# A fused patch, attention and FFN kernel: another order of turns and PSUM banks, and the repeating table for every turn

## The chip, the cores and the metric

The kernel runs on one core of one Trainium2 chip. The metric is the device time of a run in microseconds (us). TensorE is PE in the profile, VectorE is DVE, ScalarE is ACT, GpSimd is POOL, and SP is the engine that issues all DMAs of this kernel.

## The reference

64 images go through three parts, in float32 except where integers are imitated:

```python
h = conv2d(x, stem_w, stem_b, 4)                 # 84x84 -> 21x21, 96 channels
h = leaky_relu(batchnorm(h, ...))
offset = conv2d(h, off_w, off_b, 4)              # 16 taps x (y, x) for 25 positions
h = deform_conv(h, offset, dcn_w, dcn_b)         # bilinear samples, 192 channels
h = leaky_relu(batchnorm(h, ...))                # 25 tokens of 192
h = concatenate([h, txt], axis=1)                # 25 + 77 = 102 tokens an image
h = h + attn(layernorm(h))                       # 12 heads of 16, int8 values,
                                                 # integer log2 softmax over 102 keys
h = h + gelu(layernorm(h) @ w_in.T + b) @ w_out  # 192 -> 768 -> 192
```

The integer softmax quantises the scores, subtracts the maximum, splits each into a quotient and a remainder, forms `(r*(r+b)+c) * 2**(30-q)`, sums over the keys, and replaces each ratio sum/value by the next power of two.

## The kernel before, in words

The work is cut into *turns*. A turn is one stage of one image, or, for the stages named in `PER_GROUP`, of one group of four images. All data lives in SBUF in one or two copies, so a group is also the unit in which buffers are reused. The stages used below, with the line of their main instruction in the kernel before:

- PE: STEM0 and STEM1 (stem convolution of images 0, 1 and 2, 3 of a group, L1255), HTT (transpose, L1264), OFF and OFS (offsets, L1280, L1289), HAT (the distances of pixels to sample points, two matmuls into two banks, L1302), INT (interpolation, L1312 to L1316), DCN (L1331), LN1X and LN2X (transposes of the normalised tokens, L1345), V0, V1, FQ0, FQ1 (projections, L1355 to L1389), SC (scores, L1401, L1404), PV2 (probabilities times values, L1415), PV3 (output projection, L1425), FFN0 to FFN2 (first FFN matmuls, L1367, L1371), FF2 (second, L1452).
- ACT: an eviction under the name of the PE stage (STEM L723, HAT L755 and L760, LN1X L779, SC L839, PV2 L865, FQ L827 and L829), XH1 and XH2 (normalise, L798), SQ (square of the remainder, L846), LOG (L852) and PR (exp, L859) of the ratio, and FFN (GELU, L873), which stands between two table loads (L709).
- DVE: HAT (L1032) and HATW (L1039) turn distances into weights; LS1, LN1, VE1 and LS2, LN2, VE2 are the two layer norms; QKC casts queries and keys (L1086 to L1090); the softmax of an image is MAX (L1097), MXB, MXC, DST (L1121), BND, QQ, QQG, REM, EP, EXP (L1164), SUM (L1172), RCP (L1177), and, after ACT, PW (L1187) and PR (L1194); PV3 and RES give the residual (L1200, L1207); FF2 adds the FFN (L1214).
- POOL: NRM multiplies an image's exponentials by the reciprocal of their sum (L674, from RCP to LOG), OFS splits offsets into bf16 parts (L658 to L668), RS1 and RS2 are the reciprocal square roots of the layer norms (L683 to L686), WDF scales the convolution weights once (L651).
- SP: LX, LA, LR load, RP spreads the offsets to the rows that HAT reads (L603), SD packs samples (L593), PT transposes the probabilities (L587), QD places the queries in twelve DMAs (L578), YO0 and YO1 store.

In what follows NRM.2 is the turn of the third image of a group, RCP.2 its reciprocal, and so on; in the tables the number behind the point is an image of 0 to 63, and a group stage bears its last image.

Each engine walks the same text, `SLOT`: one entry per turn, with the engine, the stage and a lag in images; `run_slot` executes those of its engine for image `slot - lag`. So the order of the turns on each engine repeats every four images, and engines meet through semaphores alone. Two further tables, `OPENING` and `CLOSING`, list by hand the first and the last turns of each engine; `walk` runs those lists and leaves their turns out of the repeating part. `BANKS` gives each stage its PSUM banks, and `BankUse.take` makes PE wait until the stage that used a bank before has been evicted:

```python
def take(self, t, k, drained, per, plus=None):
    b = t.banks[k]
    if b in self.last:
        before, at = self.last[b]
        self.pe.wait_ge(before, at)
    self.last[b] = (drained, per * t.n + (per if plus is None else plus + 1))
```

Of the kernel before, what the change touches and what calls it, by code (L numbers as in the profile page):

```python
# [79 lines left out]
act.LOG.18 dve.RES.61 pe.HAT.7 dve.HATW.52 act.HAT.11 dve.LN2A.60 act.XH1.15 pe.FF2.18 dve.LS2.61  # L80
act.XH1.14 sp.PT.88 dve.PV3.60 pe.STEM0.0 pool.RS2.52 act.PR.18 dve.RES.60 dve.LS2.60 act.STEM.7
pe.LN1X.11 dve.LN2.60 act.LN1X.15 dve.VE2.60 pe.FF2.17 act.SQ.16 dve.MAX.59 dve.MXB.59 act.XH1.13
pe.LN1X.10 dve.MXC.59 sp.QD.84 act.LN1X.14 dve.DST.59 pe.HAT.6 act.XH1.12 dve.BND.59 act.STEM.6
pe.LN1X.9 dve.MAX.58 dve.QQ.59 pool.NRM.51 act.LN1X.13 pe.FF2.16 dve.MXB.58 act.HAT.10 dve.QQG.59
act.LOG.17 pe.LN1X.8 dve.MXC.58 sp.SD.80 dve.REM.59 act.LN1X.12 pe.PV2.15 dve.DST.58 act.PR.17
dve.EP.59 act.LOG.16 pe.V0.8 dve.BND.58 act.V.15 dve.MAX.57 pe.FQ0.8 dve.QQ.58 act.PR.16 dve.EXP.59
act.PV2.19 pe.FQ1.8 pool.OFS.40 sp.YO0.92 dve.QQG.58 act.FQ0.12 dve.EP.58 pe.PV2.14 dve.PREP0.4
act.FQ1.12 dve.REM.58 pe.HTT.3 act.OC.19 dve.SUM.59 act.V.14 dve.PREP2.52 pe.HAT.5 act.HAT.9
dve.MXB.57 sp.LR.84 dve.RCP.59 pe.PV3.15 act.PV2.18 dve.EXP.58 act.OC.18 dve.SUM.58 pe.INT.7
act.HAT.8 pool.NRM.50 dve.MXC.57 dve.MAX.56 pe.HAT.4 act.PV2.17 dve.DST.57 act.INT.11 pe.PV2.13  # L90
dve.BND.57 act.OC.17 sp.YO1.92 dve.QQ.57 pe.PV3.14 act.HTT.7 dve.QQG.57 dve.PREP3.52 act.INT.10
pe.INT.6 dve.MXB.56 act.PV2.16 dve.RCP.58 pe.PV3.13 act.OC.16 dve.REM.57 dve.LS1.55 act.SC.15
pool.RS1.44 pe.PV2.12 dve.LS1.54 sp.LX.72 act.STEM.5 dve.LS1.53 pe.INT.5 act.HTT.6 dve.LS1.52
act.STEM.4 dve.LN1.52 pe.PV3.12 dve.VE1.52 act.XH2.19 dve.EP.57 pe.SC.11 act.SC.14 dve.PREP1.16
act.XH2.18 dve.MXC.56 pe.STEM1.0 sp.DCN.80 dve.DST.56 act.INT.9 dve.BND.56 pe.HTT.2 act.VC.15
pool.NRM.49 dve.PW.59 act.INT.8 dve.FF2.63 pe.SC.10 act.LN2X.19 dve.QQ.56 dve.EXP.57 pe.INT.4
act.XH2.17 dve.QQG.56 act.SC.13 sp.LA.80 pe.LN2X.15 dve.PR.59 act.SQ.15 dve.FF2.62 pe.SC.9
# [15 lines left out]


OPENING = dict(
    pe="""
  STEM0.3 STEM1.3 HTT.0 HTT.1 OFF.3 OFS.3 HAT.0 STEM0.7 HTT.2 STEM1.7 HAT.1 HAT.2 HTT.3 HTT.4 HAT.3
  INT.0 INT.1 INT.2 INT.3 OFF.7 HTT.5 DCN.3 OFS.7 HTT.6 HAT.4 STEM0.11 LN1X.0 LN1X.1 HTT.7 HAT.5
  LN1X.2 LN1X.3 V0.3 FQ0.3 FQ1.3 STEM1.11 HAT.6 HTT.8 HAT.7 INT.4 INT.5 SC.0 SC.1 INT.6 SC.2 INT.7
  OFF.11 HTT.9 SC.3 OFS.11 DCN.7 V1.3 HTT.10 HAT.8 HTT.11 STEM0.15 HAT.9 LN1X.4 LN1X.5 LN1X.6 PV2.0  # L120
  LN1X.7 V0.7 FQ0.7 FQ1.7 PV2.1 HAT.10 HTT.12 PV3.0 INT.8 HAT.11 PV2.2 PV3.1 INT.9 PV3.2 PV2.3
  INT.10 PV3.3 SC.4 HTT.13 STEM1.15 SC.5 INT.11 LN2X.0 SC.6 LN2X.1 HTT.14 OFF.15 LN2X.2 V1.7 HTT.15
  LN2X.3 OFS.15 SC.7 DCN.11 FFN0.3
    """,
    act="""
  STEM.0 STEM.1 STEM.2 HTT.0 STEM.3 OFF.3 OFS.3 HAT.0 HTT.1 STEM.4 STEM.5 HAT.1 HTT.2 HTT.3 HAT.2
  HAT.3 INT.0 STEM.6 INT.1 HTT.4 INT.2 STEM.7 INT.3 OFF.7 DCN.3 OFS.7 HTT.5 HTT.6 HAT.4 XH1.0 STEM.8
  XH1.1 LN1X.0 XH1.2 LN1X.1 XH1.3 LN1X.2 HAT.5 LN1X.3 V.0 HTT.7 FQ0.3 STEM.9 V.1 FQ1.3 STEM.10 HAT.6
  HAT.7 INT.4 SC.0 SC.1 INT.5 INT.6 STEM.11 SC.2 INT.7 HTT.8 VC.0 SQ.0 OFF.11 OFS.11 HTT.9 SQ.1
  DCN.7 SC.3 HTT.10 LOG.0 V.2 VC.1 HAT.8 PR.0 SQ.2 V.3 HTT.11 STEM.12 LOG.1 XH1.4 XH1.5 STEM.13  # L130
  LN1X.4 PR.1 XH1.6 LN1X.5 SQ.3 LN1X.6 XH1.7 HAT.9 PV2.0 LN1X.7 VC.2 LOG.2 PR.2 LOG.3 V.4 PR.3 VC.3
  FQ0.7 FQ1.7 OC.0 V.5 HAT.10 PV2.1 OC.1 HAT.11 PV2.2 OC.2 INT.8 PV2.3 HTT.12 OC.3 INT.9 SC.4 VC.4
  STEM.14 HTT.13 STEM.15 SC.5 VC.5 XH2.0 XH2.1 INT.10 LN2X.0 INT.11 XH2.2 XH2.3 LN2X.1 SC.6 HTT.14
  LN2X.2 OFF.15 SQ.4 V.6 HTT.15 LN2X.3 SQ.5 V.7 VC.6 DCN.11 VC.7 SC.7
    """,
    dve="""
  PREP0.3 PREP1.3 HAT.0 HATW.0 HAT.1 HATW.1 HAT.2 HAT.3 HATW.2 HATW.3 PREP2.3 PREP3.3 LS1.0 LS1.1
  LS1.2 LS1.3 LN1.3 VE1.3 QKC.3 HAT.4 HATW.4 HAT.5 HATW.5 HAT.6 HATW.6 HAT.7 HATW.7 MAX.0 MXB.0
  MXC.0 DST.0 MAX.1 BND.0 MXB.1 QQ.0 MXC.1 QQG.0 DST.1 EP.0 BND.1 REM.0 QQ.1 MAX.2 QQG.1 MXB.2 EXP.0
  REM.1 SUM.0 EP.1 RCP.0 EXP.1 SUM.1 MXC.2 DST.2 BND.2 MAX.3 QQ.2 MXB.3 QQG.2 RCP.1 REM.2 LS1.4  # L140
  LS1.5 LS1.6 LS1.7 LN1.7 VE1.7 EP.2 MXC.3 DST.3 EXP.2 BND.3 PW.0 QQ.3 PR.0 QQG.3 EP.3 REM.3 SUM.2
  PW.1 RCP.2 EXP.3 SUM.3 RCP.3 PR.1 HAT.8 PW.2 PR.2 HATW.8 PW.3 PR.3 HAT.9 QKC.7 PV3.0 HAT.10 HATW.9
  RES.0 PV3.1 HAT.11 RES.1 LS2.0 HATW.10 LS2.1 PV3.2 RES.2 HATW.11 PV3.3 RES.3 LS2.2 LS2.3 LN2.3
  VE2.3 MAX.4 MXB.4 MXC.4 DST.4 MAX.5 BND.4 MXB.5 QQ.4 MXC.5 EP.4 QQG.4 DST.5 REM.4 BND.5 MAX.6 QQ.5
  MXB.6 QQG.5 EXP.4 REM.5 EP.5 SUM.4 EXP.5 RCP.4 SUM.5
    """,
    pool="""
  OFS.3 WDF.3 OFS.7 RS1.3 OFS.11 NRM.0 NRM.1 RS1.7 NRM.2 NRM.3 RS2.3 NRM.4
    """,
    sp="""  # L150
  LX.3 RP.3 LX.7 SD.3 LX.11 DCN.3 LA.3 RP.7 QD.3 SD.7 LR.3 RP.11 DCN.7 LA.7 LX.15 PT.0 PT.1 PT.2
  PT.3 QD.7 SD.11 DCN.11 LA.11 LX.19 LR.7
    """,
)
# [1380 lines left out]
```

## Time and profile before

| | us |
|---|---|
| median of 3 runs | 990.5 (989.36 to 991.37) |
| time of the profiled execution | 989.57 |
| its span, from first to last instruction | 987.5 |
| busy: PE, DVE, ACT, POOL | 844.2, 845.0, 777.5, 255.2 |
| mean granted TensorE clock, as a share of full speed | 0.958 |

A timeline row gives the start, the duration, the engine, the line, the operation and its tiles, and in brackets how long the engine had been idle and who ended that. Rows of the chain of waits give start, duration and what the chain went through. A duration of PE or DVE includes time in which the instruction had been issued and was held.

### The profile page before, as it was taken

The numbers are of one execution on the slowest core, as the hardware profiler recorded it, in microseconds if no ns is written. First come the engines' busy times: TensorE is split into PE (matmuls) and PEld (weight loads), VectorE is DVE, ScalarE is ACT, GpSimd is POOL, SyncE is SP. The second block draws the span as 40 slices with busy tenths as digits, with TensorE's granted clock in tenths as the row PEclk, the third lists the DMA queues.
The fourth block names the chain that finished last, engine by engine and source line by source line (L and its number), as shares of the span: only waits on it lengthen the run. The fifth ranks groups of instructions, "written<-read, shape, count | busy, mean of one in ns | idle before, by whom it ended". The sixth has DMA issues, their size and how long they took to land. (4 is left out here: it accounts for less than half of the span.)

```text
span 987.5 us, 18275 instructions
## 1 busy us (share of the span) xinstructions
PE 844.2 (85%) x5578; PEld 520.1 (53%) x5578; DVE 845.0 (86%) x1703; ACT 777.5 (79%) x1529; POOL 255.2 (26%) x248
## 2 busy tenths in 40 slices
...
## 3 DMA queue, kind: packets, MB, share of 16 engines
...
## 5 line engine op out<-in xcount | busy, mean ns | idle before, releaser
L674 POOL TENSOR_TENSOR ee_sb<-ee_sb,rs_sb 128x1020 f32<-128x1020 f32 x64 | 143.1, 2238 | 346.9 <-DVE rs_sb L1177 346.9
L1452 PE MATMUL bank<-w_out_sb,ge_sb 128*102 128x192 f32 x768 | 140.0, 333 | 23.5 <-ACT ge_sb L873 19.8
L1316 PE MATMUL bank<-hats_sb,ht_sb 127*96 127x400 f32 (+1 forms) x384 | 146.7, 520 | 0.4 <-ACT samp_sb L767 0.4
L1452 PEld LDWEIGHTS bank<-w_out_sb,ge_sb 128*102 128x102 f32 x768 | 121.9, 170 | 39.0 <-ACT ge_sb L873 29.5
L1039 DVE SCALAR_TENSOR_TENSOR hats_sb<-hats_sb 126x1600 f32<-126x1600 int32 x64 | 116.0, 1815 | 0.2
L760 ACT ACTIVATE hats_sb<-bank 126x400 int32<-126x400 f32 (+1 forms) x256 | 108.0, 520 | 0.0
L839 ACT ACTIVATE a_sb<-scores,sc_sb 128x1020 f16<-128x1020 f32 x64 | 71.0, 1110 | 46.3 <-PE scores L1404 46.3
L1164 DVE SCALAR_TENSOR_TENSOR ee_sb<-sq_sb,sc_sb,ep_sb 128x1020 f32<-128x1020 f32 x64 | 100.0, 1562 | 3.9 <-ACT sq_sb L846 3.9
L1316 PEld LDWEIGHTS bank<-hats_sb,ht_sb 127*96 127x96 f32 (+1 forms) x384 | 58.7, 166 | 68.7 <-issue 66.6
L846 ACT ACTIVATE sq_sb<-rm_sb,sc_sb 128x1020 f32<-128x1020 f16 x64 | 73.5, 1149 | 18.3 <-DVE rm_sb L1149 18.1
L1367 PE MATMUL bank<-xt_sb,w_in_sb 128*128 128x408 f32 (+1 forms) x204 | 83.5, 535 | 1.4 <-ACT xt_sb L779 1.4
L1121 DVE SCALAR_TENSOR_TENSOR m_sb<-a_sb,mx_sb 128x1020 f16<-128x1020 f16 x64 | 79.9, 1249 | 1.1
L1172 DVE TENSOR_REDUCE ss_sb<-ee_sb 128x10 f32<-128x1020 f32 x64 | 77.5, 1210 | 1.0
L852 ACT ACTIVATE ee_sb<-ee_sb 128x1020 f32<-128x1020 f32 x64 | 67.9, 1062 | 10.9 <-POOL ee_sb L674 10.8
L683 POOL TENSOR_TENSOR xshift_sb<-mv_sb,xshift_sb 102x4 f32<-102x4 f32 (+1 forms) x33 | 8.6, 260 | 262.5 <-DVE ve_sb L1079 261.1
L1345 PE MATMUL bank<-ident_sb,xh_sb 102*128 102x102 f32 x256 | 49.7, 278 | 23.6 <-ACT xt_sb L779 19.3
L859 ACT ACTIVATE rr_sb<-ee_sb 128x1020 uint16<-128x1020 f32 x64 | 68.3, 1067 | 1.7 <-DVE p_sb L1187 1.1
L1331 PE MATMUL bank<-wdcn_sb,samp_sb 128*100 128x192 f32 x384 | 65.1, 326 | 0.0
L873 ACT ACTIVATE ge_sb<-bank,b_in_sb 128x408 f32<-128x408 f32 (+1 forms) x102 | 51.9, 580 | 14.4 <-PE bank L1371 14.0
L1331 PEld LDWEIGHTS bank<-wdcn_sb,samp_sb 128*100 128x100 f32 x384 | 61.3, 167 | 0.0
L779 ACT ACTIVATE xt_sb<-bank 128x204 f32<-128x204 f32 x128 | 44.3, 346 | 18.7 <-PE bank L1345 18.6
L1345 PEld LDWEIGHTS bank<-ident_sb,xh_sb 102*128 102x128 f32 x256 | 31.3, 149 | 51.9 <-ACT xh_sb L798 31.5
...
## 6 DMA issues: line engine op xcount, KB each, us to landing
...
q_sb<-qb_sb SPq DMA_DIRECT2D x192, 12.8 KB, 1.9
...
```

Of the source, the lines that this page charges most:

```text
L674: nc.gpsimd.tensor_tensor(EE[b][:], EE[b][:], RS[b][:].unsqueeze(2).to_broadcast([128, RT, TOK]), ALU.mult).then_inc(scaled_done, 1)
L760: nc.scalar.activation(HATS[t.i][0:rows, 1 + j, :].bitcast(i32), bank[t.banks[1]][0:rows, 0:SMP], ACT.Abs, scale=ONE_Y, bias=-line * ONE_Y ...
L846: nc.scalar.activation(SQ[:], RM[:], ACT.Square, bias=sc[:, NHALFB:NHALFB + 1]).then_inc(sq_done, 1)
L1039: v.scalar_tensor_tensor(hat[:, 1:, :], hat[:, 1:, :].bitcast(i32), -ONE_Y, hat[:, 0:1, :].to_broadcast([rows, NCH, SMP]), ALU.add, ALU.mu ...
L1121: v.scalar_tensor_tensor(M16[b][:], A16[b][:], MAGIC16 + 128.0, MX[b][:].unsqueeze(2).to_broadcast([128, RT, TOK]), ALU.min, ALU.subtract) ...
L1164: v.scalar_tensor_tensor(EE[b][:].rearrange("p h k -> p (h k)"), SQ[:], sc[:, CC:CC + 1], EP[:].bitcast(bf16), ALU.add, ALU.mult).then_inc ...
L1172: v.tensor_reduce(SS[b][:], EE[b][:], AX.X, ALU.add).then_inc(ss_done, 1)
L1316: last = mm(dst, HT[0:rows, t.i, j, :], HATS[t.i][0:rows, 1 + j, :], start=(j == 0 and not odd), stop=(j == NCH - 2 and odd == 1))
L1331: last = mm(dst, SAMP[:, k, :, :].rearrange("c g p -> c (g p)"), WD[:, k, :], start=False, stop=(k == PACKED - 1))
L1345: last = nc.tensor.transpose(bank[t.banks[0]][:, c * TOK:(c + 1) * TOK], xh[b][:, 64 * c:64 * c + 128], ident[0:TOK, 0:TOK])
L1367: mm(bank[t.banks[first + c]][:, 0:n], weights(k + c, c), src[:, c, :], start=True, stop=False)
L1452: last = mm(bank[t.banks[0]][0:TOK, 0:D], GE[:, f, t.i * TOK:(t.i + 1) * TOK], WOUT[:, f, :], start=(f == 0), stop=(f == FT - 1))
```

## The change

`OPENING`, `CLOSING`, `turns_of` and `run_turn` go. `walk` runs only the repeating table, from the first slot to the last, so the first and last turns come in its order too. The table itself is another one, and so are the banks:

```diff
 SLOT = """
-dve.PR.62 act.V.16 pe.HTT.4 dve.FF2.64 act.LN2X.21 dve.HAT.55 pe.LN2X.17 act.VC.16 dve.PW.61
...
+dve.DST.59 act.V.14 pe.PV2.23 dve.BND.59 act.OC.18 dve.MAX.58 pe.LN1X.19 act.PV2.17 dve.QQ.59
...
-BANKS = dict(FFA=(0, 1, 2, 3), STEM0=(3, 2), STEM1=(2, 1), HTT=(5,), OFF=(3,), OFS=(0,),
-             HAT=(3, 0), INT=(4, 3), DCN=(3,), LN1X=(1,), LN2X=(1,), V0=(3, 4), V1=(4, 2),
-             FQ0=(0, 5), FQ1=(3, 1), PV2=(2,), PV3=(1,), FFN0=(4, 5), FFN1=(2, 1), FFN2=(0, 3),
-             FF2=(5,))
+BANKS = dict(FFA=(2, 0, 1, 5), STEM0=(5, 4), STEM1=(0, 1), HTT=(3,), OFF=(4,), OFS=(2,),
+             HAT=(0, 3), INT=(2, 4), DCN=(4,), LN1X=(5,), LN2X=(1,), V0=(0, 4), V1=(0, 5),
+             FQ0=(3, 5), FQ1=(0, 2), PV2=(1,), PV3=(5,), FFN0=(3, 2), FFN1=(4, 5), FFN2=(0, 1),
+             FF2=(2,))
...
-def run_slot(engine, slot, stages, apart):
+def run_slot(engine, slot, stages):
     for of_engine, stage, lag in PHASES[slot % GRP]:
-        n = slot - lag
-        if of_engine == engine and 0 <= n < IMG and (stage, n) not in apart:
-            run_turn(engine, stage, n, stages)
+        n, per_group = slot - lag, stage in PER_GROUP
+        if of_engine == engine and 0 <= n < IMG:
+            stages[stage](Turn(n // GRP if per_group else n, n % GRP, per_group,
+                               BANKS.get(stage)))
...
-    opening, closing = turns_of(OPENING, name), turns_of(CLOSING, name)
-    for stage, n in opening:
-        run_turn(name, stage, n, stages)
     for slot in range(FIRST_SLOT, LAST_SLOT + 1):
-        run_slot(name, slot, stages, {*opening, *closing})
-    for stage, n in closing:
-        run_turn(name, stage, n, stages)
+        run_slot(name, slot, stages)
```

In a few stages the waits in front of one instruction are written in another order (`xt1`, `xt2`, `quotient`, `exp_int`, `pixels_first`, `interpolate`, `weigh_v`), and PE's `stem` waits for its pixels only behind the wait for its first bank. No instruction that computes or moves data is added or removed.

PE around the first scores of a group, in the middle of the program. Before (L1425 is PV3, L1401 and L1404 are SC, L1255 is STEM1):

```order
L1415 MATMUL bank<-pt_sb,v_sb 32x102 x12
L1316 MATMUL bank<-hats_sb,ht_sb 96x400 x3
L1425 MATMUL bank<-wproj_sb,o_sb 102x192 x3
L1401 MATMUL scores<-kk_sb,q_sb 128x102 x7
L1404 MATMUL scores<-kk_sb,q_sb 128x102 x4
L1255 MATMUL bank<-xc_sb,stem_w_sb 96x441 x2
```

Now:

```order
L1313 MATMUL bank<-pt_sb,v_sb 32x102 x12
L1162 MATMUL bank<-ident_sb,h_sb 126x96 x4
L1214 MATMUL bank<-hats_sb,ht_sb 96x400 x3
L1299 MATMUL scores<-kk_sb,q_sb 128x102 x7
L1302 MATMUL scores<-kk_sb,q_sb 128x102 x4
L1323 MATMUL bank<-wproj_sb,o_sb 102x192 x3
L1153 MATMUL bank<-xc_sb,stem_w_sb 96x441 x2
```

The output projection of the group's last image, PV3.3, has moved from in front of the scores SC.0 to behind them.

ACT behind the GELUs, in the middle of the program. Before (L846 is SQ.2, L852 LOG.1, L755 and L760 HAT.0, L798 XH1.0 and XH1.1, L859 PR.1, L723 STEM.0, L779 LN1X.0, and L846 SQ.3):

```order
L846 ACTIVATE sq_sb<-rm_sb,sc_sb 128x1020
L852 ACTIVATE ee_sb<-ee_sb 128x1020
L755 ACTIVATE hats_sb<-bank 126x400
L760 ACTIVATE hats_sb<-bank 126x400 x4
L798 ACTIVATE xh_sb<-xa_sb,xshift_sb,rstd_sb 102x192 x2
L859 ACTIVATE rr_sb<-ee_sb 128x1020
L723 ACTIVATE h_sb<-bank 96x441
L779 ACTIVATE xt_sb<-bank 128x2x102
L846 ACTIVATE sq_sb<-rm_sb,sc_sb 128x1020
```

Now:

```order
L743 ACTIVATE sq_sb<-rm_sb,sc_sb 128x1020
L651 ACTIVATE hats_sb<-bank 126x400
L656 ACTIVATE hats_sb<-bank 126x400 x4
L619 ACTIVATE h_sb<-bank 96x441
L749 ACTIVATE ee_sb<-ee_sb 128x1020
L695 ACTIVATE xh_sb<-xa_sb,xshift_sb,rstd_sb 102x192 x2
L756 ACTIVATE rr_sb<-ee_sb 128x1020
L674 ACTIVATE xt_sb<-bank 128x2x102
L743 ACTIVATE sq_sb<-rm_sb,sc_sb 128x1020
```

The stem eviction STEM.0 has moved from behind XH1.0, XH1.1 and PR.1 to in front of them and of LOG.1; the turns between the two squares are the same.

POOL at the start of the program, behind its fills. Before:

```order
L658 TENSOR_TENSOR offp_sb<-offt_sb,later_sb 96x100
L661 TENSOR_TENSOR offr_sb<-offt_sb,offp_sb 96x100
L663 TENSOR_TENSOR offp_sb<-offr_sb,later_sb 96x100
L668 TENSOR_TENSOR offs_sb<-offr_sb,offp_sb 96x100
L651 TENSOR_TENSOR wdcn_sb<-wdcn_sb,ee_sb 128x2304
```

Now:

```order
L547 TENSOR_TENSOR wdcn_sb<-wdcn_sb,ee_sb 128x2304
L554 TENSOR_TENSOR offp_sb<-offt_sb,later_sb 96x100
L557 TENSOR_TENSOR offr_sb<-offt_sb,offp_sb 96x100
L559 TENSOR_TENSOR offp_sb<-offr_sb,later_sb 96x100
L564 TENSOR_TENSOR offs_sb<-offr_sb,offp_sb 96x100
```

The one scaling of the convolution weights, WDF, has moved ahead of the first group's offsets.

## Rows read from the trace of the kernel before

**Rows 1.** Windows by stage: busy us and count of each engine, clock, DMA share.
```profile
core 0: us, PE busy (x) PEld busy (x) DVE busy (x) ACT busy (x) POOL busy (x), PEclk, DMA share, GB/s
0.00:120.00 120.00, 76.58 (x392) 40.18 (x392) 74.21 (x151) 48.58 (x109) 26.55 (x38) 0.91 0.24 61
241.00:783.00 542.00, 499.14 (x3446) 311.48 (x3447) 508.90 (x1010) 476.84 (x945) 149.93 (x140) 1.00 0.26 57
...
900.00:987.00 87.00, 57.53 (x317) 38.21 (x317) 43.18 (x101) 45.41 (x73) 11.63 (x13) 0.74 0.14 30
```

**Rows 2.** Chain of waits, two groups four apart (start, us, what).
```profile
603.62 0.89 PE bank L1371 x4
...
820.45 0.89 PE bank L1371 x4
```

**Rows 3.** Chain of waits within one group.
```profile
666.09 1.15 ACT sq_sb L846
...
673.65 2.90 DVE ee_sb L1164
...
683.65 1.33 SPq L587
...
692.77 1.86 DMA q_sb<-qb_sb
```

**Rows 4.** Timeline of PE around the first scores.
```profile
693.83 0.41 PE L1425 MATMUL bank<-wproj_sb,o_sb 128*102 128x192 bf16 x3
694.67 0.49 PE L1401 MATMUL scores<-kk_sb,q_sb 128*128 128x102 bf16 x7 [0.43 <-DMA q_sb<-qb_sb]
```

**Rows 5.** Timeline of DVE from RCP.2 to HAT.0.
```profile
673.29 0.21 DVE L1177 RECIPROCAL rs_sb<-ss_sb 128x10 f32<-128x10 f32 x1
673.65 2.89 DVE L1164 SCALAR_TENSOR_TENSOR ee_sb<-sq_sb,sc_sb,ep_sb 128x1020 f32<-128x1020 f32 x1 [0.16 <-ACT sq_sb L846]
...
678.24 0.35 DVE L1214 TENSOR_TENSOR y_sb<-bank,x_sb 102x192 f32<-102x192 f32 x1
678.51 1.79 DVE L1032 TENSOR_SCALAR hats_sb<-hats_sb 126x400 f32<-126x400 f32 x1
```

**Rows 6.** Timeline of POOL, the same stretch: NRM.2 and NRM.3.
```profile
673.58 1.89 POOL L674 TENSOR_TENSOR ee_sb<-ee_sb,rs_sb 128x1020 f32<-128x1020 f32 x1 [7.56 <-DVE rs_sb L1177]
678.13 1.95 POOL L674 TENSOR_TENSOR ee_sb<-ee_sb,rs_sb 128x1020 f32<-128x1020 f32 x1 [2.66 <-DVE rs_sb L1177]
```

**Rows 7.** Line L1164 in ten groups: ns minimum, median, maximum.
```profile
L1164 DVE SCALAR_TENSOR_TENSOR ee_sb<-sq_sb,sc_sb,ep_sb x40: 1210/1273/2894, 269.3 to 781.8; 128x1020 f32<-128x1020 f32 x40
```

**Rows 8.** Timeline of DVE in the opening, the same turns.
```profile
129.96 0.21 DVE L1177 RECIPROCAL rs_sb<-ss_sb 128x10 f32<-128x10 f32 x1
130.08 1.22 DVE L1164 SCALAR_TENSOR_TENSOR ee_sb<-sq_sb,sc_sb,ep_sb 128x1020 f32<-128x1020 f32 x1
...
133.26 2.05 DVE L1032 TENSOR_SCALAR hats_sb<-hats_sb 126x400 f32<-126x400 f32 x1
```

**Rows 9.** Timeline of ACT from XH1.0 to SQ.3.
```profile
670.00 1.01 ACT L798 ACTIVATE xh_sb<-xa_sb,xshift_sb,rstd_sb 102x192 f32<-102x192 f32 x2
...
671.82 0.54 ACT L723 ACTIVATE h_sb<-bank 96x441 f32<-96x441 f32 x1
672.24 0.35 ACT L779 ACTIVATE xt_sb<-bank 128x204 f32<-128x204 f32 x1
672.46 1.16 ACT L846 ACTIVATE sq_sb<-rm_sb,sc_sb 128x1020 f32<-128x1020 f16 x1
```

**Rows 10.** Timeline of the first 75 us: offsets, weights, first HAT.
```profile
20.93 0.35 POOL L658 TENSOR_TENSOR offp_sb<-offt_sb,later_sb 96x100 bf16<-96x100 f32 x1 [4.38 <-ACT offt_sb L746]
...
22.64 1.69 SPq L603 DMA_DIRECT2D rx_sb<-offs_sb  x2
...
25.72 5.04 POOL L651 TENSOR_TENSOR wdcn_sb<-wdcn_sb,ee_sb 128x2304 f32<-128x2304 f32 x1 [3.11 <-DVE dcn_bias_parts_sb L951]
...
30.94 0.59 PE L1302 MATMUL bank<-rx_sb,lines_sb 9*126 9x400 bf16 x2 [10.53 <-DMA rx_sb<-offs_sb]
...
40.54 0.37 DVE L1032 TENSOR_SCALAR hats_sb<-hats_sb 126x400 f32<-126x400 f32 x1
```

**Rows 11.** Timeline of DVE in the opening: the wait for the first queries and keys.
```profile
86.03 0.58 DVE L1086 CAST qb_sb<-qk_sb 128x816 bf16<-128x816 int8 x1 [14.16 <-ACT qk_sb L829]
```

**Rows 12.** Timeline of DVE in the last group: EXP.61.
```profile
924.11 1.28 DVE L1164 SCALAR_TENSOR_TENSOR ee_sb<-sq_sb,sc_sb,ep_sb 128x1020 f32<-128x1020 f32 x1 [1.99 <-ACT sq_sb L846]
```

More of the change, by code:

```diff
@@ L80 @@
[L80 to L97, printed above, removed]
```

149 lines of the change are left out of this document (39 added, 110 removed).

## Prediction

> **What bounds the kernel now.** I read the windows first. In ten full groups, from 241 to 783 us, DVE is busy 508.90 us, PE 499.14 and ACT 476.84 of 542 [rows 1]: 50.9, 49.9 and 47.7 us in a group. The chain of waits then gives the length of a group: it passes the same FFN matmuls at 603.62 and, four groups on, at 820.45 [rows 2], so 216.83 / 4 = 54.2 us. No engine is full; what sets 54.2 is a loop through all of them. The reader is to see its stations within one group [rows 3]: the GELUs end, ACT squares image 2's remainder at 666.09, DVE forms EXP.3 at 673.65, the last PR turn of the group ends and SP issues the transpose PT at 683.65, then the twelve query DMAs, the last of which lands at 692.77 + 1.86 = 694.6. PE starts the scores at 694.67, 0.43 us after it had become free [rows 4]; they lead through PE's turns to the next FFN matmuls.
>
> The second thing to see is inside DVE's time. EXP takes 1.27 us as a rule, but 2.89 at 673.65 [rows 5], and of 40 in ten groups the median is 1.273 and the maximum 2.894 [rows 7]. The slow one was issued at 673.65, just behind NRM.2 on POOL at 673.58 [rows 6]. HAT.0, at 678.51, takes 1.79 us against 0.37 in the opening [rows 5, 10], and it lies under NRM.3, from 678.13 to 680.08 [rows 6]. So where DVE starts second it is held until POOL is done: 2.89 - 1.27 = 1.6 and 1.79 - 0.37 = 1.4 us, both on the loop. In the opening the same turns stand tighter: RCP.2 at 129.96, EXP.3 at 130.08 with 1.22 us, because EXP started first and POOL waited [rows 8].
> That POOL and DVE hold each other up by order of start is also what the Trainium skill says (SBUF — State Buffer, Who interferes with whom): whoever issues first keeps the shared port pair for the whole instruction and the other fully blocks. By that rule, and the trace agrees with its 2.89 against 1.22 us, a DVE turn that gets in front does not make the conflict vanish but hands it to POOL.
>
> **The change, part by part.** As many instructions of each kind run as before; only order, banks and the places of waits differ. Most of the table is the old one: the groups lag each other by the same number of rounds on every engine. I work through what moved on the loop, per group.
>
> 1. *PV3.3 behind SC.0 on PE.* It lengthens PE's way from the scores to the FFN by its own 0.41 us [rows 4]. Before, it lay in front of a 0.43 us wait for the queries and cost nothing. Behind it on DVE wait PV3.3's scaling, RES.3, LS2.3, the moments and the variance; these 1.9 us no longer fill the time in which DVE awaits SC.0. DVE has about 1 us of waits to give (0.31, 0.50 and 0.16 us in that group, the last one in [rows 5]), so it becomes late by some tenths at RCP.0, and NRM.0, LOG.0 and the GELUs with it. Bounds: 0 (if another turn holds the GELUs anyway) to 1.3 us (the whole way through DVE). I take 0.5, near PE's row, since both ways end in the same GELU.
>
> 2. *STEM.0 in front of LOG.1 and XH1.0 on ACT.* XH1.0, and with it LN1X.0, FF2.2 and RCP.2, comes later by one stem eviction, by start to start 672.24 - 671.82 = 0.42 us [rows 9]. Cost +0.4. SQ.3 does not come later, since the same turns lie between SQ.2 and SQ.3.
>
> 3. *What 2 does to EXP.3.* Before, RCP.2 started at 673.29 and SQ.3 was done at 673.62, so EXP.3 started 0.36 us behind RCP.2, and NRM.2 had come 0.07 us before it [rows 5, 6, 9]. Now RCP.2 is 0.42 later against SQ.3. The square is done 0.33 - 0.42 = 0.1 us ahead of RCP.2, and EXP.3 follows 0.12 us behind the start of RCP.2, as in the opening [rows 8], ahead of POOL, which came 0.29 us behind it. From RCP.2 to the end of the HAT turn it was 680.30 - 673.29 = 7.01 us [rows 5]; in the opening, without FF2.3, it was 135.31 - 129.96 = 5.35 [rows 8]; with FF2.3's 0.27, by start to start [rows 5], 5.62. Gain 1.4 us. The HAT turn there is now HAT.1 and is held just as HAT.0 was. Bounds: 0 (still held) to 1.6 (the whole hold). NRM.2 is late by the 1.1 us that EXP.3 keeps it, yet LOG.2 and LOG.3 stand behind HAT.1 on ACT and are not reached earlier.
>
> 4. *STEM0 and HAT.0 ahead of FF2.0 on PE, LX ahead of SD on SP, QKC directly behind PR.3, HAT.0 earlier on DVE.* STEM0 and HAT.0 now fill the time in which PE awaits the GELUs. QD waits for the transpose at 683.65 [rows 3] and not for QKC, so QKC gains nothing. LX's two issues fall into time in which SP waits for samples. Zero each. What costs it if that cover goes: PE's 1.0 us for STEM0, once a group.
>
> 5. *Banks.* LN1X gets bank 5, HTT bank 3, FF2 bank 2. I went through each bank's previous user; every one is evicted before PE comes, except HAT.1's, which waits for HAT.0's evictions about where PE would otherwise wait for XH1.0. Zero.
>
> A group: +0.5 + 0.4 - 1.4 = -0.5 us. I take -0.4, since the two orders of start must hold every time. The middle has about 14 such groups: -5.6 us.
>
> 6. *Opening.* WDF now stands ahead of the first offsets on POOL. It can't start before 25.72 and takes 5.04 us, to 30.8; the four offset turns (20.93 to 22.6) come after it, to 32.5; RP's issue of 1.69 ends at 34.2 [rows 10]. In the second group the rows land 2.3 us after such an issue, so the first HAT matmul comes at 36.5 to 36.8 instead of 30.94: +5.8. Most of it is covered: DVE takes up HAT.0 only at 40.54, behind its own constants [rows 10]. What is left is the fourth image's chain, with HTT.4, HTT.5 and STEM1 now ahead of INT.3: about +2 us on the first tokens. Against that HAT.4 and HATW.4, behind QKC before, fall into DVE's 14.16 us wait [rows 11]: up to 2.2 us. Sum +1.5; bounds -1 and +5.8.
>
> 7. *Closing.* EXP.61 waited 1.99 us for a square that stood behind GELUs in the list [rows 12]; in the table the square comes first, but the GELUs later. The last four FF2 turns wait for each other's adds as before. I take -0.5, bounds -2.5 and +3.
>
> **Sum.** 989.57 - 5.6 + 1.5 - 0.5 = 985.0 us. The profiled execution lies 0.9 us under the median of 990.5 and within the runs' spread; I leave the number as it is.
>
> **The rivals.**
>
> *A, slower: EXP.3 stays second.* If SQ.3 comes 0.3 us later against RCP.2 than I reckon (the 0.29 us between RCP.2 and NRM.2 less the 0.12 of EXP.3, plus 0.1), NRM.2 is first again and the 1.4 us are not won, while 1 and 2 are paid: +0.9 us in each of 14 groups. Place: DVE at RCP.2. 989.57 + 12.6 + 1.5 - 0.5 = 1003 us. For it: the margin is small and was missed by 0.07 us before. Against it: the opening shows the other order in this very kernel [rows 8]. Chance 0.32.
>
> *B, a wash: the opening is not covered.* Then the 5.8 us of 6 arrive whole: 989.57 - 5.6 + 5.8 - 0.5 = 989.3. For it: the clock is at 0.91 of full speed in the first 120 us [rows 1], so the later start may meet slow matmuls. Against it: DVE's start at 40.54. Chance 0.19.
>
> *C, faster still: 1 costs nothing and PE's filled wait is a gain of its own.* Then a group saves 0.4 - 1.4 = -1.0: 989.57 - 14 + 1 = 976.6. For it: PE stands idle before FF2.0 and before SC.0 in every group. Against it: the loop goes through ACT there. Chance 0.12.
>
> **How the numbers follow.** The forecast, 985.0 with a range of its own of 980 to 989, has the remaining 0.37. No change means within 0.2%, 2 us, about what a measurement of this kernel can tell. Of the forecast's case 0.33 lie under 988.5 and 0.04 above; C gives 0.12 faster; B splits 0.03, 0.11, 0.05; A gives 0.02 same and 0.30 slower. Sums: faster 0.48, same 0.17, slower 0.35. The range reaches from C's time to just over A's, 976 to 1004; beyond it lie sums of several errors.
>
> **What would show it.** In the changed profile: the chain's period between equal FFN rows, 53.8 if right, 55.1 for A, 53.2 for C. L1164's counterpart with a maximum near 1.3 us instead of 2.9, and NRM.2 rows of 2.8 us in place of 1.9. DVE idle in front of the PV3.3 scaling by 1 to 2 us in each group. The first HAT matmul near 36.7 us, and the first SC within 2 us of where it was (97.98). I am wrong if EXP.3 keeps its 2.9 us, if the period moves by more than 1 us, or if opening and closing together move by more than 4 us.

## The result, and the profile after

The changed kernel takes 976.43 us (median of 4 runs, 975.82 to 977.48) against 990.93 (4 runs), a ratio of 0.9853 with a 95% interval of 0.9838 to 0.9867. That is faster by 14.5 us; I had forecast 5.5. The profiled execution took 977.03 us with a span of 974.9, 12.5 us under the one before.

The windows of the profile after, as [rows 1] before:

```profile
0.00:120.00 120.00, 71.37 (x396) 38.43 (x396) 76.08 (x156) 49.49 (x110) 26.92 (x38) 0.84 0.24 62
241.00:783.00 542.00, 502.78 (x3509) 314.71 (x3507) 499.92 (x1021) 488.26 (x967) 167.25 (x140) 1.00 0.28 59
...
900.00:975.00 75.00, 51.45 (x274) 34.06 (x274) 39.43 (x82) 41.99 (x69) 13.16 (x12) 0.77 0.13 29
```

In the same 542 us more instructions run on PE, DVE and ACT, and yet DVE is busy 9 us less: its holds went. POOL is busy 17 us more for the same 140 instructions: it is the one that is held now.

The chain of waits, two equal stations (DCN) four groups apart, as [rows 2]:

```profile
588.93 3.90 PE bank L1229 x24
...
802.06 3.90 PE bank L1229 x24
```

213.13 / 4 = 53.3 us a group. Line L1061 (EXP), ten groups, as [rows 7]:

```profile
L1061 DVE SCALAR_TENSOR_TENSOR ee_sb<-sq_sb,sc_sb,ep_sb x40: 1219/1274/1278, 266.9 to 770.7; 128x1020 f32<-128x1020 f32 x40
```

The maximum fell from 2894 to 1278 ns: no EXP is held any more. The timeline of DVE from RCP.2 on, as [rows 5] (L1074 is RCP, L1061 EXP.3, L929 HAT.1, L1084 PW.2):

```profile
664.01 0.20 DVE L1074 RECIPROCAL rs_sb<-ss_sb 128x10 f32<-128x10 f32 x1
664.14 1.22 DVE L1061 SCALAR_TENSOR_TENSOR ee_sb<-sq_sb,sc_sb,ep_sb 128x1020 f32<-128x1020 f32 x1
...
667.58 1.78 DVE L929 TENSOR_SCALAR hats_sb<-hats_sb 127x400 f32<-127x400 f32 x1
669.78 0.43 DVE L1084 TENSOR_SCALAR p_sb<-rr_sb 128x1020 bf16<-128x1020 uint16 x1 [0.42 <-ACT rr_sb L756]
```

And POOL, as [rows 6]: NRM.2 and NRM.3 in one row.

```profile
664.30 4.84 POOL L570 TENSOR_TENSOR ee_sb<-ee_sb,rs_sb 128x1020 f32<-128x1020 f32 x2 [4.86 <-DVE rs_sb L1074]
```

EXP.3 starts 0.13 us behind RCP.2 and 0.16 us ahead of NRM.2, and takes 1.22 us; the two NRM take 4.84 us together, where they took 1.89 and 1.95. HAT.1, which lies under NRM.3, is held as HAT.0 was. The last row of DVE is new: DVE waits for ACT there. The timeline of ACT shows why, from SQ.2 to the last PR (first, middle and last rows; between them ACT never waits):

```profile
656.41 1.15 ACT L743 ACTIVATE sq_sb<-rm_sb,sc_sb 128x1020 f32<-128x1020 f16 x1
657.46 0.48 ACT L651 ACTIVATE hats_sb<-bank 126x400 f32<-126x400 f32 x1
...
668.64 1.11 ACT L756 ACTIVATE rr_sb<-ee_sb 128x1020 uint16<-128x1020 f32 x1
669.59 1.11 ACT L749 ACTIVATE ee_sb<-ee_sb 128x1020 f32<-128x1020 f32 x1
...
670.74 1.11 ACT L756 ACTIVATE rr_sb<-ee_sb 128x1020 uint16<-128x1020 f32 x1
```

From these timelines I took one start in each group: the eviction of SC.0, SQ.2, RCP.2, the last PR turn on DVE (PR.3), and the next SC.0. Means over ten groups, the fourth to the thirteenth, in us:

| kernel | SC.0 to SQ.2 | SQ.2 to RCP.2 | RCP.2 to PR.3 | PR.3 to SC.0 | group |
|---|---|---|---|---|---|
| before | 24.79 | 7.20 | 9.91 | 12.52 | 54.42 |
| changed | 24.90 | 7.60 | 8.76 | 12.25 | 53.52 |

Over the whole run: the first SC.0 is evicted at 98.78 us before and 97.59 after, the last at 908.62 and 896.50, and the span ends at 987.5 and 974.9. So the opening gained 1.2 us, the fifteen groups between 10.9, and the closing 0.4. By stretch, summed over the fifteen groups: SC.0 to SQ.2 grew by 0.9 us, SQ.2 to RCP.2 by 6.1, RCP.2 to PR.3 shrank by 13.8, and PR.3 to SC.0 by 4.1. RCP.2 to PR.3 shrank less than fifteen full holds would give, since before EXP.3 was held in twelve of the fifteen groups only (in the first and the last two it took 1.22 us).

Three signs that the prediction named came: the group took 53.3 us by the chain (forecast 53.8), NRM.2 takes 2.81 us in every full group instead of 1.89, and DVE is idle in front of PV3.3's scaling by 0.8 to 1.9 us in every full group, where it had not been idle at all.

### The profile page after: what moved, and what is told of

It reads as the page before. It is cut to its first block, busy times and chain, and to the rows that moved or that the text cites. A ratio compares the mean times of both kernels' runs of the same rounds, so it can differ in the third digit from the quotient of the medians.

```text
span 974.9 us, 18274 instructions
## 1 busy us (share of the span) xinstructions
PE 827.3 (85%) x5578; PEld 514.0 (53%) x5578; DVE 826.7 (85%) x1703; ACT 780.1 (80%) x1529; POOL 281.7 (29%) x248
## 4 chain that ended last, share of the span: by engine, by line
PE 35%; ACT 18%; SPq 15%; issue 13%; DVE 11%; DMA 5%; POOL 2%; ACTq 0%; DVEq 0%; POOLq 0%
SPq L474 11%; PE bank L1265 7%; PE bank L1229 5%; PE bank L1269 4%; ACT hats_sb L656 4%; DMA q_sb<-qb_sb 3%; PE bank L1214 3%; ACT ee_sb L749 3%; SPq L483 2%; ACT xt_sb L674 2%; PE scores L1299 2%; PE bank L1178 2%; ACT rr_sb L756 2%; ACT xh_sb L695 1%; PE bank L1243 1%
## 5 line engine op out<-in xcount | busy, mean ns | idle before, releaser
L570 POOL TENSOR_TENSOR ee_sb<-ee_sb,rs_sb 128x1020 f32<-128x1020 f32 x64 | 159.6, 2503 | 182.3 <-DVE rs_sb L1074 182.3
L1350 PE MATMUL bank<-w_out_sb,ge_sb 128*102 128x192 f32 x768 | 138.0, 329 | 12.8 <-DVE y_sb L1111 9.1
L1214 PE MATMUL bank<-hats_sb,ht_sb 127*96 127x400 f32 (+1 forms) x384 | 143.6, 510 | 1.1 <-DVE hats_sb L936 1.1
L579 POOL TENSOR_TENSOR xshift_sb<-mv_sb,xshift_sb 102x4 f32<-102x4 f32 (+1 forms) x33 | 20.2, 611 | 308.2 <-DVE ve_sb L976 308.2
L1214 PEld LDWEIGHTS bank<-hats_sb,ht_sb 127*96 127x96 f32 (+1 forms) x384 | 58.1, 164 | 66.0 <-issue 64.4
L1061 DVE SCALAR_TENSOR_TENSOR ee_sb<-sq_sb,sc_sb,ep_sb 128x1020 f32<-128x1020 f32 x64 | 80.7, 1261 | 0.0
L1018 DVE SCALAR_TENSOR_TENSOR m_sb<-a_sb,mx_sb 128x1020 f16<-128x1020 f16 x64 | 77.8, 1215 | 0.6
L554 POOL TENSOR_TENSOR offp_sb<-offt_sb,later_sb 96x100 bf16<-96x100 f32 x16 | 11.6, 725 | 155.1 <-ACT offt_sb L642 155.1
```

The lines of the kernel that those rows point to most:

```text
L570: nc.gpsimd.tensor_tensor(EE[b][:], EE[b][:], RS[b][:].unsqueeze(2).to_broadcast([128, RT, TOK]), ALU.mult).then_inc(scaled_done, 1)
L1061: v.scalar_tensor_tensor(EE[b][:].rearrange("p h k -> p (h k)"), SQ[:], sc[:, CC:CC + 1], EP[:].bitcast(bf16), ALU.add, ALU.mult).then_inc ...
L1214: last = mm(dst, HT[0:rows, t.i, j, :], HATS[t.i][0:rows, 1 + j, :], start=(j == 0 and not odd), stop=(j == NCH - 2 and odd == 1))
L1350: last = mm(bank[t.banks[0]][0:TOK, 0:D], GE[:, f, t.i * TOK:(t.i + 1) * TOK], WOUT[:, f, :], start=(f == 0), stop=(f == FT - 1))
```

## The experiments

Ratios are to the kernel before, run on the same chip. In the edits a table entry is written as the turn it stands for, and the turns stand in the order in which the engine takes them.

### The hand lists alone

```diff
-    opening, closing = turns_of(OPENING, name), turns_of(CLOSING, name)
+    opening, closing = [], []
```

> The kernel before, with its own repeating table and banks, but without the two hand lists. Theory 'middle' (the gain of the change comes from the order inside the full groups, and the lists are worth about what the profile after shows at the two ends: first scores 1.2 us earlier, last 0.5 us): 987 to 991 us, the mean length of a group stays 54.0 us and EXP.3 keeps its 2.9 us. Rival 'ends' (the hand lists cost the 14 us): 976 to 980. Rival 'lists earn': 993 or more.

Measured: 989.62 us against 990.56 (0.9993, 0.9977 to 1.0009). The lists are worth at most about 2 us either way. The gain lies in the repeating part: its order of turns, its banks and its waits.

### EXP.3 first, in the kernel before

```diff
 ACT: ... SQ.2 LOG.1 HAT.0 XH1.0 XH1.1 PR.1
-STEM.0 LN1X.0 SQ.3
+LN1X.0 SQ.3 STEM.0
```

> The kernel before with one turn moved in the repeating part: ACT evicts STEM.0 behind SQ.3 and no longer ahead of LN1X.0, so SQ.3 is done 0.42 us earlier against RCP.2. Theory (EXP.3 then starts ahead of NRM.2, and from there ACT, which works without a pause from SQ.2 to PR.3, is the limit): every EXP in full groups takes 1.2 to 1.3 us, RCP.2 to RCP.3 falls from 4.54 to 2.6 us, SQ.2 to the last PR of the group from 17.1 to 16.4, a group is 0.75 us shorter, 978 to 982 us. Rival A (EXP.3 is still second): 990 to 992. Rival B (the whole 1.9 us reach the query transfers): 965 to 970.

Measured: 980.78 us, 0.9914 (0.9893 to 0.9935). One moved turn brings 9.8 of the 14.5 us; by the spans of the profiled executions it is 11.8 of 12.5 (975.7 against 987.5 and 974.9). DVE in this kernel (L1177 RCP.2, L1164 EXP.3, L1187 PW.2):

```profile
664.95 0.21 DVE L1177 RECIPROCAL rs_sb<-ss_sb 128x10 f32<-128x10 f32 x1
665.07 1.22 DVE L1164 SCALAR_TENSOR_TENSOR ee_sb<-sq_sb,sc_sb,ep_sb 128x1020 f32<-128x1020 f32 x1
...
671.11 0.43 DVE L1187 TENSOR_SCALAR p_sb<-rr_sb 128x1020 bf16<-128x1020 uint16 x1 [0.81 <-ACT rr_sb L859]
```

EXP.3 leads, and then DVE awaits ACT by 0.81 us. SQ.2 to PR.3 is 16.36 us (7.20 + 9.16), the same as in the changed kernel (7.60 + 8.76), although RCP.2 comes 0.4 us earlier here. So ACT sets this stretch once the hold is gone: 0.75 us of the 1.9 arrive, as the first theory had it.

### EXP.3 second, in the changed kernel

```diff
 ACT: ... LN1X.0
-SQ.3 XH1.2
+XH1.2 SQ.3
```

> The changed kernel with one turn moved: ACT squares SQ.3 behind XH1.2 and no longer ahead of it, 0.44 us later. RCP.2 doesn't depend on it. Theory (order of start at DVE and POOL): EXP.3 comes about 0.1 us after NRM.2 and is held, 2.9 us, in every full group; the group is 0.75 us longer, 985 to 989 us. Rival (0.44 us of lateness and no more, or hidden by ACT): 976 to 980.

Measured: 996.45 us, 1.0057 (1.0037 to 1.0077): slower even than before. DVE and POOL in it (L1061 EXP.3, L570 NRM.2):

```profile
674.22 1.89 POOL L570 TENSOR_TENSOR ee_sb<-ee_sb,rs_sb 128x1020 f32<-128x1020 f32 x1 [4.85 <-DVE rs_sb L1074]
674.39 2.80 DVE L1061 SCALAR_TENSOR_TENSOR ee_sb<-sq_sb,sc_sb,ep_sb 128x1020 f32<-128x1020 f32 x1 [0.25 <-issue]
```

POOL leads by 0.17 us and EXP.3 takes 2.80 us. RCP.2 to PR.3 goes back to 9.91 us, 1.15 more than in the changed kernel, where I had expected 0.75: RCP.3 comes 1.9 us later, DVE no longer waits for ACT's PR, and RCP.2 keeps the 0.4 us of its later place. In the fifteen groups from the first SC.0 to the last the kernel is 15.3 us longer. This is rival A, made to happen. Its price was 20 us by the medians but 14 by the profiled executions (991.22 against 977.03): the median of this kernel is 5 us above its profiled execution, and I can't say what the other runs lost.

### PV3.3 back ahead of SC.0

```diff
 PE: ... INT.2
-SC.0 PV3.3
+PV3.3 SC.0
```

> The changed kernel with PV3.3 back in front of SC.0 on PE, where it was before. My prediction had +0.5 us a group for its place behind SC.0; by that this kernel takes 969 to 972 us. What the profile after shows (SC.0 to LOG.0 is only 0.3 us longer than before, SC.0 to SQ.2 0.1) speaks for 974 to 977. If PE's place ahead of SC.0 is now full (PE waited only 0.2 us for the queries there), SC.0 comes later and it is 977 to 981.

Measured: 972.80 us, 0.9826 (0.9803 to 0.9848). The same kernel measured once more, on another chip, whose expectation was

> The changed kernel with PV3.3 ahead of SC.0, once more, on the chip of its neighbours. SC.0 to LOG.0 is 16.33 us in each full group instead of 16.73 by the earlier profile; 15 groups of 0.40 are 6 us at most. If the gain is real: 971 to 975. If it was chance: 976 to 979.

took 972.38 us, 0.9799 (0.9780 to 0.9818). SC.0 to LOG.0 is 16.33 us in an ordinary group and 16.73 in the changed kernel: 0.40 us, PE's 0.41 of [rows 4]. Up to SQ.2, 0.32 us of it are left (24.46 against 24.78), 4.8 us in fifteen groups; the medians are 3.6 and 6.3 us under the two of the changed kernel. PE in this kernel, L1323 being PV3.3:

```profile
627.18 0.41 PE L1323 MATMUL bank<-wproj_sb,o_sb 128*102 128x192 bf16 x3
627.47 0.49 PE L1299 MATMUL scores<-kk_sb,q_sb 128*128 128x102 bf16 x7
```

SC.0 follows without a wait. This is the fastest kernel of the study. Of its two intervals the first just touches that of the changed kernel, the second lies below both.

### The weights behind the offsets on POOL

```diff
-POOL: WDF OFS.3
+POOL: OFS.3 WDF
```

> The changed kernel with POOL's WDF back behind the first group's offsets, as before. The first HAT matmul comes at about 31 us instead of 36. My prediction had DVE, which takes up HAT.0 only at 40.5 us, cover most of it, with 2 us left on the first tokens: by that 974 to 976. What the profile after shows (first tokens 0.5 us later, HAT.2's and HAT.3's evictions awaited 0.8 and 1.3 us by DVE) says 975 to 977. Rival B of the prediction (the 5 us arrive whole at the end): 970 to 972.

Measured: 979.47 us, 0.9880 (0.9858 to 0.9903). The changed kernel as it is, measured once more on another chip,

> The changed kernel as it is, once more, as the reference of its neighbours on the same chip: 975.8 to 978. If the kernels with old waits or later weights are really slower, this one stays under 978; if their 3 to 5 us are the chip's or chance, this one comes out at 979 to 982 too.

took 978.70 us, 0.9872 (0.9850 to 0.9894). The two can't be told apart. But the experiment took back less than it was meant to: the offsets were ready 10 us earlier, and the first HAT matmul started at 32.98 us and not at 31, against 36.05 in the changed kernel and 30.94 before. DVE took up HAT.0 at 40.65 instead of 40.93 and the first tokens (LS1) at 70.91 instead of 70.61, so these 3 us are wholly covered; that the whole 5 us are is the likely reading and was not tried. The two medians of the changed kernel, 976.43 and 978.70, also show that it moves by 2 us from one measurement to the next.

### Waits in the old order

All of the moved waits back, on every engine:

> The changed kernel with the waits of xt1, xt2, quotient, exp_int, pixels_first, interpolate, weigh_v and stem in the order of before; turns and banks are those of the change. I costed the wait order at nothing: 975 to 978. Rival (a wait that is met last but stands first makes the instruction start later): each group's parts are longer by 0.05 us a wait or more, 979 or above.

Measured: 981.83 us, 0.9912 (0.9891 to 0.9933): as long as the rival said, but not in its way, since an ordinary group's SC.0 to SQ.2 is 24.79 us beside 24.78. In two groups, from 313.0 and from 848.9 us on, the granted clock was 0.50 for 3.4 us. On PE alone:

> The changed kernel with the old order of waits on PE alone (pixels_first, interpolate, weigh_v, stem). In the kernel with all old waits the ordinary group was as long as in the changed kernel (SC.0 to SQ.2 24.78 us in both), and the 4 us more of the profiled run lay in single groups, 1.9 of them in one in which PE's clock fell to half for 3.4 us. If PE's wait order makes such dips: a dip in the middle again and 980 us or more. If it is chance: no dip, and within 1.5 us of the changed kernel on the same chip.

Measured: 985.11 us, 0.9944 (0.9926 to 0.9962), beside the 978.70 of the changed kernel on that chip. No dip of the clock in the middle, and slower all the same: neither case as I wrote it. Then the two halves, and the new order of PE's waits in the kernel before, of which this is the part in `interpolate` (those of `stem`, `pixels_first` and `weigh_v` moved likewise):

```diff
 def interpolate(t):
+    free.take(t, odd, samp_done, 1)
     pe.wait_ge(w_done, t.count(1, 1))
     pe.wait_ge(ht_done, t.count(1, 1))
-    free.take(t, odd, samp_done, 1)
```

> The changed kernel with the old order of waits in PE's interpolate and weigh_v alone. If these are the costly ones (both come several times between the last PR and the next SC.0, the stretch that was 0.3 us longer with old waits): 983 to 986. If not: 976 to 979.

> The changed kernel with the old order of waits in PE's stem and pixels_first alone: the complement of its neighbour. 983 to 986 if these are the costly ones, else 976 to 979; if both are in between, each has a part, and if both are under 980 the 6 us need all four or were one build's.

> The kernel before, with its own turns, banks and lists, and PE's waits (stem, pixels_first, interpolate, weigh_v) in the order of the change. With the old order on PE the changed kernel took 985.1 instead of 978.7 us on one chip, though an undisturbed group was equally long. Theory 'waits' (the wait order alone is worth some 5 us in either kernel, and is what my prediction lacked): 983 to 987. Rival 'turns' (it is worth something only with the new order of turns, or the 6 us were this one build's): 988.5 to 992.

Measured: 989.00 us with the old waits in interpolate and weigh_v (0.9951, 0.9927 to 0.9976; its runs spread from 981.83 to 990.62), 979.30 with those in stem and pixels_first (0.9876), and 993.42 for the kernel before with the new order (1.0025, 1.0009 to 1.0041). So three kernels with the old waits in interpolate and weigh_v lie above the changed kernel, but by very different amounts: about 10 us beside the 979.30 on the same chip, 6 with all four of PE's old waits, and only 2 with every old wait on every engine (981.83 beside 979.47 and 979.98, two other variants of the changed kernel on its chip). In the first, five of nine runs took 989.0 to 990.6 us and four 981.8 to 984.5; the profile is of one of the four, so what the slower ones lost is not known. An undisturbed group is as long with either order: from PR.3 to SC.0 11.74 to 11.78 us with the old waits, 11.75 in the changed kernel. The mean of that stretch over fifteen groups is 12.57 with the old waits of the two functions, but 12.39 with all the old waits, and 12.31 in the changed kernel. What the order of waits does there is not shown.

In the kernel before, the new order of PE's waits brings nothing, and the 2 us that it cost have a place in the trace: SC.0 to LOG.0 took 17.8 to 17.9 us in three groups instead of one. The next experiment is about those groups.

### XH2.0 behind SC.1, in the kernel before

```diff
 ACT: SC.0 STEM.2 HTT.1 STEM.3
-XH2.0 SC.1
+SC.1 XH2.0
```

> The kernel before with one turn moved: ACT evicts SC.1 ahead of XH2.0 and no longer behind it. In the profile before, in one group XH2.0 waited 1.67 us for POOL's RS2, whose last piece took 1.27 us instead of 0.20 because DVE's DST had started 0.02 us ahead of it, and SC.0 to LOG.0 was 17.8 us instead of 16.4. Theory: no group of the full ones is above 16.9 us from SC.0 to LOG.0, the common ones stay at 16.4 or fall a little; 987 to 990 us. Rival (SC.1 isn't on the way to LOG.0): groups with 17.7 us remain.

Measured: 988.36 us, 0.9970 (0.9952 to 0.9988). SC.0 to LOG.0 is at most 16.91 us in full groups, where the kernel before had 17.76 in one and the one without lists in three. POOL's last piece of RS2 was held in one group here too (1.26 us), and the stretch stayed at 16.67. The three rows of the kernel before on which this rests:

```profile
534.30 1.22 DVE L1121 SCALAR_TENSOR_TENSOR m_sb<-a_sb,mx_sb 128x1020 f16<-128x1020 f16 x1
534.32 1.27 POOL L686 TENSOR_TENSOR xshift_sb<-xshift_sb,rstd_sb 102x4 f32<-102x4 f32 x1
535.62 0.55 ACT L798 ACTIVATE xh_sb<-x_sb,xshift_sb,rstd_sb 102x192 f32<-102x192 f32 x1 [1.67 <-POOL xshift_sb L686]
```

POOL's last piece of RS2, 0.20 us by itself, started 0.02 us behind DVE's DST and was held for all of it; ACT's XH2.0, and the scores behind it, waited. The new table has XH2.0 behind SC.1, and is free of this.

### One eviction out of ACT's full stretch

```diff
 PE: PV3.3 ahead of SC.0, and PV2.0 behind FQ1
 ACT: STEM.1 behind PR.3
-V0=(0, 4), PV2=(1,), INT=(2, 4)
+V0=(0, 1), PV2=(4,), INT=(2, 1)
```

> The changed kernel with PV3.3 ahead of SC.0, and with ACT's eviction STEM.1 moved behind PR.3; for its bank PE's PV2.0 goes behind FQ1, and V0, PV2 and INT get other banks (0 and 1, 4, 2 and 1). Theory (from SQ.2 to PR.3 ACT works without a pause and is the limit since EXP.3 starts first, so each eviction taken out of that stretch shortens the group by its 0.42 us): RCP.3 to PR.3 5.7 instead of 6.13 us, a group of 52.15 instead of 52.57 without a fetch, 966 to 970 us. Rival (the queries' DMAs wait for QKC, which ACT's FQ evictions release at the same time as before): 971 to 974.

Measured: 1046.49 us, 1.0585 (1.0552 to 1.0617). Neither case. The timeline of PE, INT.3 (L1210, L1212, L1214), and its windows (the columns of [rows 1]):

```profile
682.01 0.54 PE L1210 MATMUL bank<-hats_sb,ht_sb 63*96 63x400 f32 x1 [1.72 <-ACT h_sb L619]
...
682.86 3.94 PE L1214 MATMUL bank<-hats_sb,ht_sb 127*96 127x400 f32 x6
```

```profile
676.00:680.30 4.30, 4.26 (x37) 2.32 (x35) 3.67 (x12) 2.54 (x5) 0.00 (x0) 1.00 0.23 49
680.30:682.90 2.60, 0.89 (x5) 0.32 (x5) 2.50 (x7) 2.37 (x5) 1.75 (x3) 0.99 0.63 176
682.90:686.30 3.40, 3.40 (x7) 1.48 (x7) 3.37 (x8) 0.50 (x1) 0.00 (x0) 0.50 0.03 8
```

INT's odd images now share bank 1 with STEM1, whose eviction PE has to await: 1.72 us in each group. In the group shown the granted clock is 0.50, 1.2 GHz, for 3.4 us right behind that pause, and six matmuls take 3.94 us instead of 2.25. From 150 to 880 us there are twelve such falls; nine come right at that pause, three some 15 us ahead of it, and four of the pauses have none behind them. Also the query casts came at 47.0 us after SC.0 instead of 42.0, since ACT stood at PV2.0's eviction. RCP.3 to PR.3 did fall, from 6.1 to 5.9, but the experiment as built cost 70 us beside it, of which the pause, the falls of the clock and the later casts are what the trace shows; that all of it comes from the choice of banks was not tried by itself.

### Where the query transfers meet an instruction fetch

The stretch from PR.3 to SC.0 holds the same work in every group and yet takes 11.7 to 13.2 us. In twelve profiles I took the middle thirteen groups of each. In 108 groups a 16 KB instruction packet (queue q8) starts between 10.6 and 1.5 us ahead of SC.0, and the stretch takes 12.52 us on average; in the 48 others 11.98, 32 of them 11.73 to 11.84. (A second instruction queue, q14, has 55 packets of 8 KB, which this count leaves out.) In the changed kernel the chain of waits has the landing of the last query DMA in two groups, one of either kind:

```profile
414.96 2.99 DMA q_sb<-qb_sb
...
522.95 1.87 DMA q_sb<-qb_sb
```

and the DMA view of 414.9 to 418.0 us has the row below, which that of 522.9 to 526.0 has not:

```profile
q8 instruction: 1, 0.02, 2.6%
```

The Trainium skill (Runtime: NRT & Kernel Launch, Instruction fetch mechanics) says that instructions come in blocks of 16 KiB, or 256 instructions; the packets' size agrees. To move the fetches by half a block I put 64 one-column matmuls on PE into its wait for the first offsets.

> The changed kernel with 64 one-column matmuls more on PE ahead of the first HAT turn, while PE awaits the offsets; each brings a weight load, 128 instructions in all. They cost nothing there by themselves. Theory (a group whose query transfers meet a 16 KB instruction fetch of PE loses 0.5 to 1.2 us from PR.3 to SC.0): the fetches come half of their spacing earlier in PE's work, so the groups that lose are others: those of 11.8 us from PR.3 to SC.0 are again those without a fetch in the last 10 us ahead of SC.0, and are no longer groups 7 to 10. Time within 975 to 980. Rival (the group's number or the data decides): groups 7 to 10 again have 11.8 us.

Measured: 979.98 us, 0.9886 (0.9859 to 0.9913), and the fetches stayed nearly where they were; groups 7 to 10 (counted from 0) again take 11.8 us, as the rival had it. The trace shows why nothing moved. The 64 calls became 128 matmuls and 128 weight loads, as the view of their line in this kernel has it (count, then ns minimum, median and maximum):

```profile
L1193 PEld LDWEIGHTS bank<-ident_sb x128: 74/76/77, 32.8 to 35.9; 1*1 1x1 f32 x128
L1193 PE MATMUL bank<-ident_sb x128: 158/158/159, 32.8 to 35.9; 1*1 1x1 f32 x128
```

That is 256 instructions, one whole block and not half of one, and the run has 47 packets of 16 KB where the changed kernel has 46. So the experiment could not decide what it was built for. It does speak for these packets being PE's own instructions.

The other traces have a better test. In sixteen profiles (all but that of the experiment before this one), group 6 has a packet in the stretch in twelve, and takes 12.48 us or more; in the other four, both of PV3.3 ahead, the one without lists and the one with XH2.0 behind SC.1, it has none and takes 11.74 to 11.76. So the number of the group does not decide it. That the fetch causes the delay is supported by this, the two landings and the count; no experiment moved a fetch alone, so it is not shown.

## Why the prediction fell short

The sign and the mechanism of step 3 held; the size didn't: 14.5 us, of which I had 5.5. What failed are terms of the sum. By the two profiled executions, in us over the whole run:

| term | forecast | measured | by |
|---|---|---|---|
| step 1, SC.0 to SQ.2 | +7.0 (14 times 0.5) | +0.9 | 369.07 to 369.92 us in fifteen groups |
| steps 2 and 3, SQ.2 to PR.3 | -14.0 (14 times -1.0) | -7.6 | 252.03 to 244.39 |
| steps 4 and 5 and the waits, PR.3 to SC.0 | 0 | -4.1 | 188.73 to 184.59 |
| discount | +1.4 | none | |
| step 6, opening | +1.5 | -1.2 | 98.78 to 97.59 |
| step 7, closing | -0.5 | -0.4 | 78.84 to 78.41 |
| sum, before rounding | -4.6 | -12.5 | |

So step 1 was priced far too high for its stretch, steps 4 and 5 with the waits were put at nothing where 4.1 us went, and the opening was given the wrong sign; steps 2 and 3 were put too high by about as much as step 1, and it is luck that these two errors cancel. In place of the missing terms the runs show this: one moved turn (EXP.3 first) brings nearly the whole gain alone, in the kernel before. The 4.1 us of PR.3 to SC.0 lie in disturbed groups and stay open.

**Step 1, PV3.3 (+0.5 a group): right in price.** The stretch up to LOG.0 is 0.40 us longer by it. But I took it for the whole of what happens between SC.0 and SQ.2. Of the 0.40 us 0.32 reach SQ.2, and the stretch grew by only 0.11 in the mean (24.64 to 24.78 in an ordinary group), so other moves gave back some 0.2 us. XH2.0 behind SC.1, which spares the groups in which POOL lost to DST, is one of them: the one such group among the ten of the table is worth 0.13 in their mean. I hadn't looked at it.

**Step 2, STEM.0 (+0.4): right in its row, wrong in the sum.** RCP.2 comes 7.60 us behind SQ.2 instead of 7.20. It does not reach PR.3, as the kernel before with EXP.3 first has the same 16.36 us from SQ.2 to PR.3 without it.

**Step 3, EXP.3 (-1.4): the mechanism right.** The hold of 1.6 us went in every group that had it, by the 0.16 us that I had put at 0.17 (0.29 less 0.12). RCP.2 to PR.3 fell by 1.15, not 1.4, since DVE now awaits ACT's PR.2 by 0.42 us. Steps 2 and 3 together: forecast -1.0, measured 0.40 - 1.15 = -0.75. What the prediction drew from the Trainium skill (SBUF — State Buffer, Who interferes with whom), that the conflict is handed to the one that starts second, held: POOL needs 4.84 us for its two NRM instead of 3.84.

**Step 4 (zero) and step 5, banks (zero).** PR.3 to SC.0 is 0.27 us shorter in the mean. An undisturbed group has the same 11.75 us in both kernels, so the 0.27 lie in how many groups are disturbed and by how much: the packets of the fetch fall into the stretch in twelve of the fifteen groups before and in nine now. That is a coincidence of places and no term that I could have summed. The order of waits may bear on it too; I had costed the waits at nothing without looking at each, and the runs don't agree on what they are worth. The same order gives nothing in the kernel before, so it can't be added as a term of its own. Banks cost nothing visible here, but this table was made with them: where INT's odd images shared a bank with STEM1, PE waited 1.72 us for it in each group.

**The discount.** I took -0.4 where the sum was -0.5, and counted 14 groups where there are 15 from first scores to last. Measured, -0.73 in each of 15.

**Step 6, opening (+1.5; measured -1.2).** The first tokens came 0.5 us later (LS1 at 70.61 against 70.11), not 2; the query casts 1.1 us later (87.10 against 86.03, [rows 11]); and from there to SC.0 the 2.2 us came back as I had reckoned. In the repeated changed kernel the first SC.0 is at 98.73, so the opening lies between 1.2 us gained and nothing. The part that failed is the +2 us for the chain of the fourth image: it showed as 0.5 at the first tokens.

**Step 7, closing (-0.5): measured -0.4.**

**The rivals.** C had the time, 976.6, for a wrong reason: step 1 did cost its 0.4 us up to LOG.0, and 2 and 3 brought 0.75 and not 1.0 in a group. A lay nearer than its 0.32: the reserve is 0.16 us, and one turn moved by 0.44 us brought it about.

In us: the groups gave 10.9 instead of 5.6, the opening 1.2 instead of a loss of 1.5, the closing 0.4; that is the 12.5 between the spans. The rest to 14.5 is the 2 us by which the two profiled runs stand differently to their medians (1.4 under, 0.6 over).
